# Differential attention in two 64-row halves, with the stacks of terms written to DRAM and one causal mask moved to GpSimd

## The chip, the cores and the metric

The kernel runs on one core of a Trainium2 chip. The metric is the device time of one execution in microseconds (us), the median of several executions. The engines are TensorE (PE, with its weight loads as PEld), VectorE (DVE), ScalarE (ACT), GpSimd (POOL) and SyncE (SP), whose queue (SPq) issues all DMA transfers of this kernel.

## The reference

Sixteen sequences of 256 tokens and 256 channels pass through eight sublayers: four pairs of an attention and a feed-forward part, each behind a layer norm and with a gated residual. The change touches the third sublayer, called L1_attn: a differential attention with 32 heads of 8 channels, whose softmaxes are subtracted in pairs.

```
scaling = HD ** (-0.5)
q = (x @ Wq).reshape(b, t, 2 * H, HD).transpose(0, 2, 1, 3) * scaling
k = (x @ Wk).reshape(b, t, 2 * H, HD).transpose(0, 2, 1, 3)
v = (x @ Wv).reshape(b, t, H, 2 * HD).transpose(0, 2, 1, 3)
scores = jnp.einsum('bhqd,bhkd->bhqk', q, k)
causal = jnp.triu(jnp.full((t, t), -jnp.inf, dtype=jnp.float32), 1)
aw = jax.nn.softmax((scores + causal).astype(jnp.float32), axis=-1)
...
aw = aw.reshape(b, H, 2, t, t)
aw = aw[:, :, 0] - lam * aw[:, :, 1]
attn = jnp.einsum('bhqk,bhkd->bhqd', aw, v)
attn = attn * jax.lax.rsqrt(jnp.mean(attn * attn, axis=-1, keepdims=True) + 1e-05)
...
return attn @ Wo
```

## The kernel before

Each sublayer is a loop of slots over the 16 sequences (`slots`); all residual rows X stay in SBUF. Every engine has its own program for the slot, and semaphores tie them together. A step for a later sequence stands in an earlier slot: in slot i of L1_attn, k and q are projected for sequence i+1, the maxima are taken for sequence i, the second half of the heads (groups gg 4 to 7) of sequence i-1 is finished, and then the first half (gg 0 to 3) of sequence i is taken up to its values product.

The scores are computed twice, from bf16. Each f32 q and k is split into three bf16 parts (`split_qk` on POOL, qk_parts), the parts go to DRAM (qk_dram, L2232), and 24 transfers of 8 rows each bring them back into the stacks QS and KS (L2249): six products of parts, 8 channels each, are 48 contraction rows for one head of a pair, and rows 64 to 111 hold the other head of the pair. QS has a separate column block for each head of the pair, with zeros in the other head's rows, so that all matmuls contract over 128 rows. Two more transfers (L2251) clear three rows for the maximum.

- `max_scores` (PE, L1881 to L1890) makes the scores with queries on partitions, for four heads: one bank with the first query tile, two banks with the second; `later4` is added by a matmul with the identity as the causal mask. `maxima` (DVE, L2105) takes the negated row maxima, `split_max` (POOL, L2196 to L2202) splits them into three bf16 parts, `max_T` (PE, L1898) transposes them, ACT copies them to maxT (L2025), and SP writes them into three rows of QS (`l1a_max_sync`, L2263: six transfers for each half of the heads).
- `exp_scores` (PE, L1920 to L1927) makes the scores again with keys on partitions, now with the maximum subtracted by the matmul itself, and the mask `earlier4`; ACT takes the exponent (`exps`, L2036) into pw (first key tile, 256 queries) and pz (second key tile, 128 queries).
- `values` (PE, L1942 and L1944) multiplies with v in 32-column pieces; `by_token` transposes to tokens and DVE divides (L2113, L2115); `subtract`, squares (POOL, L2213), mean (DVE), the power -0.5 (POOL, L2217), `norm`, `normed_T`, `out` (L1971), `gated` (DVE, L530) and `add_to_x` (POOL, L535) end the sublayer for the sequence. `ln_rstd` (POOL, L485 and L487) belongs to the layer norm of a later sequence.

The order of work on an engine is only the order of the calls in its `slot`. On SP a slot is: the gate's transfer (L522), the parts of sequence i+1 to DRAM (`l1a_sync`), then, behind a wait for the first maxT of sequence i, six L2263 transfers, 26 transfers for the stacks of sequence i+1 (`l1a_stack_sync`), and, behind the second maxT, six more L2263 transfers.

## Time and profile before

| | us |
|---|---|
| three runs, median | 2285.53 |
| three runs, lowest to highest | 2275.45 to 2287.73 |
| the profiled execution | 2258.67 |
| its span | 2256.8 |

| engine | busy us | share of the span |
|---|---|---|
| PE | 1910.5 | 85% |
| PEld | 1418.4 | 63% |
| DVE | 1373.3 | 61% |
| POOL | 896.1 | 40% |
| ACT | 762.5 | 34% |

The busy shares are means over eight sublayers with different limits. L1_attn covers about 643 to 1420 us of the span. The mean granted clock of TensorE is 0.925 of full speed over the span. In the rows further on, a timeline has the start in us, the duration in us, the engine, the line, the operation, what is written and read, how many, and in brackets how long the engine had stood idle and on whose account.

### The profile page before, as it was taken

The numbers are of one execution on the slowest core, as the hardware profiler recorded it, in microseconds if no ns is written. First come the engines' busy times: TensorE is split into PE (matmuls) and PEld (weight loads), VectorE is DVE, ScalarE is ACT, GpSimd is POOL, SyncE is SP. The second block draws the span as 40 slices with busy tenths as digits, with TensorE's granted clock in tenths as the row PEclk, the third lists the DMA queues.
The fourth block names the chain that finished last, engine by engine and source line by source line (L and its number), as shares of the span: only waits on it lengthen the run. The fifth ranks groups of instructions, "written<-read, shape, count | busy, mean of one in ns | idle before, by whom it ended". The sixth has DMA issues, their size and how long they took to land.

```text
span 2256.8 us, 41632 instructions
## 1 busy us (share of the span) xinstructions
PE 1910.5 (85%) x13912; PEld 1418.4 (63%) x13912; DVE 1373.3 (61%) x3587; ACT 762.5 (34%) x1575; POOL 896.1 (40%) x917
## 2 busy tenths in 40 slices
PE   8999997899956887888898967798986787998887
PEld 5655554789944666566666645576765666886343
DVE  4777775565523554445445534688874676887775
ACT  2444443122212454444454534011112222443332
POOL 0354455665541344333443422133334222664333
PEclk9999998999988999899999989799999888999787
DMA  6100000100025344334433430000000100000011
GB/s 221 41 8 7 5 7 8 32 8 9 10 38 108 48 62 63 49 61 56 64 65 54 66 57 5 10 10 7 9 21 27 36 14 21 10 14 15 28 36 43
DMA packets 116497, 82.05 MB, mean 36 GB/s; under 512 B 10524, under 2 KB 113676, under 8 KB 116108
## 3 DMA queue, kind: packets, MB, share of 16 engines
q1 hardware_dynamic: 116364, 80.22, 17.6%
q8 instruction: 91, 1.49, 0.3%
q14 instruction: 42, 0.34, 0.1%
HBM read 62.49 MB, written 16.91 MB: 35 GB/s over the span
## 4 chain that ended last, share of the span: by engine, by line
PE 54%; SPq 16%; DVE 16%; issue 6%; DMA 4%; POOL 2%; ACT 1%; DVEq 1%; POOLq 0%; ACTq 0%
PE PS L1017 15%; SPq L2249 10%; SPq L2263 5%; DMA QS<-maxT 3%; PE PS L665 3%; PE PS L722 2%; PE PS L1172 2%; PE PS L738 2%; DVE xn L494 2%; PE PS L504 2%; PE PS L1920 2%; PE PS L719 2%; PE PS L1889 1%; PE PS L689 1%; PE PS L1942 1%
## 5 line engine op out<-in xcount | busy, mean ns | idle before, releaser
L2105 DVE TENSOR_REDUCE negmax<-PS 128x2 f32<-128x512 f32 (+1 forms) x384 | 241.3, 684 | 275.7 <-PE PS L1884 275.1
L535 POOL TENSOR_TENSOR X<-X,y_sb 128x512 f32 (+1 forms) x128 | 165.4, 1292 | 205.9 <-DVE y_sb L530 200.9
L2036 ACT ACTIVATE pw<-PS 128x512 f32<-128x512 f32 x256 | 140.1, 595 | 261.9 <-PE PS L1921 261.5
L530 DVE TENSOR_TENSOR y_sb<-PS,ga_sb 128x512 f32<-128x512 f32 x96 | 66.4, 692 | 245.5 <-PE PS L1971 71.9
L1920 PE MATMUL PS<-QS,KS 128*128 128x256 bf16 x512 | 104.8, 285 | 89.5 <-DMA QS<-maxT 89.5
L1017 PE MATMUL PS<-we_hi,h_parts 128*128 128x512 f32 x512 | 177.0, 406 | 0.0
L494 DVE TENSOR_SCALAR xn<-X,mv,rs 128x256 f32 (+1 forms) x256 | 157.7, 657 | 22.8 <-POOL rs L487 21.5
L514 ACT ACTIVATE hT<-PS,modT 128x256 f32<-128x256 f32 x256 | 130.0, 558 | 108.9 <-PE PS L504 107.8
L1017 PE MATMUL PS<-l_h_parts,lut_hi 128*128 128x256 f32 (+1 forms) x768 | 143.0, 288 | 6.7 <-POOL l_h_parts L1140 6.7
L485 POOL TENSOR_TENSOR rs<-mv,eps 128x2 f32<-128x2 f32 x128 | 26.8, 210 | 297.3 <-DVE mv L478 297.1
L1506 DVE SCALAR_TENSOR_TENSOR l_acc<-PS,rt_g,l_acc 128x256 f32<-128x256 f32 x256 | 105.9, 475 | 25.6 <-PE PS L1017 21.7
L1017 PEld LDWEIGHTS PS<-l_h_parts,lut_hi 128*128 128x128 f32 (+1 forms) x768 | 115.6, 181 | 9.3 <-issue 5.2
L1920 PEld LDWEIGHTS PS<-QS,KS 128*128 128x128 bf16 x512 | 51.8, 101 | 107.5 <-issue 57.5
L1017 PEld LDWEIGHTS PS<-we_hi,h_parts 128*128 128x128 f32 x512 | 97.4, 190 | 25.3 <-issue 5.3
L1017 PE MATMUL PS<-l_h_parts,lut_lo 128*128 128x256 f32 (+1 forms) x384 | 108.8, 283 | 0.0
L504 PE MATMUL PS<-ident,xn 128*128 128x128 f32 x512 | 81.2, 282 | 32.5 <-DVE xn L494 32.5
L1889 PE MATMUL PS<-KS,QS 128*128 128x256 bf16 x512 | 107.8, 288 | 1.1 <-ACT l_vpad L2066 0.3
L1017 PE MATMUL PS<-we_lo,h_parts 128*128 128x512 f32 x256 | 101.5, 397 | 0.0
L1890 PE MATMUL PS<-later,ident_b 128*128 128x128 bf16 x512 | 98.7, 228 | 0.0
L1172 PE MATMUL PS<-hT,l_wqkv 128*128 128x256 f32 x384 | 94.2, 397 | 4.9 <-ACT hT L514 4.0
L487 POOL TENSOR_TENSOR rs<-rs,half 128x2 f32<-128x2 f32 x128 | 94.2, 736 | 10.0
L1921 PE MATMUL PS<-earlier,ident_b 128*128 128x128 bf16 x512 | 97.4, 227 | 0.0
(270 smaller groups left out, 4806.4 us busy)
## 6 DMA issues: line engine op xcount, KB each, us to landing
ga_sb<-ga_dram SPq DMA_DIRECT2D x128, 128.0 KB, 2.9
qk_dram<-qk_parts SPq DMA_DIRECT2D x16, 768.0 KB, 4.1
QS<-qk_dram SPq DMA_DIRECT2D x192, 64.0 KB
KS<-qk_dram SPq DMA_DIRECT2D x192, 64.0 KB
wmod<-in_wmod SPq DMA_DIRECT2D x4, 1536.0 KB, 13.4
y_out<-X SPq DMA_DIRECT2D x16, 256.0 KB, 2.2
...
```

What stands on the lines that cost most here:

```text
L494: last_ = dve.tensor_scalar(xn[b.par][:, t, :], xb(b)[:, t, :], mv[b.par][:, t, 0:1], rs[b.par][:, t:t + 1], ALU.subtract, ALU.mult)
L504: last_ = pe.transpose(PS[:, 0, kh * T + t * P:kh * T + (t + 1) * P], xn[b.par][:, t, kh * P:(kh + 1) * P], ident[:, :])
L514: last_ = act.activation(hT[b.par][:, kh, :], PS[:, 0, kh * T:(kh + 1) * T], ACT.Identity, bias=modT[:, sub, 0, kh, bass.ds(b.n, 1)], scal ...
L535: pool.tensor_tensor(xb(b), xb(b), y_sb[b.par][:, :, :], ALU.add).then_inc(s.x.sem, 1)
L1017: last_ = pe.matmul(out, x.bitcast(F32R), y.bitcast(F32R), start=start and n == 0, stop=stop and n == 2)
L1172: last_ = pe.matmul(bank(1 + n)[:, m * T:(m + 1) * T], l3_wqkv[:, kh, n * D + m * P:n * D + (m + 1) * P], hT[b.par][:, kh, :], start=kh == ...
L1889: pe.matmul(o, q_of(b, h, P, T), k_of(b, h, 0, T), start=True, stop=False)
L1920: pe.matmul(o, k_of(b, h, 0, P), q_of(b, h, 0, T), start=True, stop=False)
L2036: act.activation(to.rearrange("p a n -> p (a n)"), bank(4 + n), ACT.Exp).then_inc(s.prob.sem, 1)
L2105: dve.tensor_reduce(to, src, AX.X, ALU.max, negate=True).then_inc(s.max.sem, 1)
L2249: sp.dma_start(to, src).then_inc(stack_in[i.par], 16)
L2263: sp.dma_start(QS[b.par][r0:r0 + 1, 8 * half_:8 * half_ + 8, pr, :], maxT[half_][r1:r1 + 8, :])\
```

## The change

Only L1_attn is changed, and the place of the first feed-forward part's buffers in SBUF.

- The rows of Wq and Wk are permuted, so that the parts of one half of the heads lie on 64 neighbouring partitions. `l1a_sync` writes the stacks whole to DRAM, all six terms, with the repeats that the six products need: 12 transfers a slot in place of one. `l1a_stack_sync` then reads them with four transfers of 48 rows (in place of 24 of 8 rows and two of zeros), and `l1a_max_sync` needs two transfers for each half in place of six.
- QS loses its doubled columns. `max_pair` and `exp_pair` work on two heads (pr 0 and 1) with contraction over 48 or 64 rows each, one in partitions 0 to 63 and one in 64 to 127, alternating, and into two different banks. A unit is a bank; a pair of units comes at once, and three banks rotate.
- The mask of the second key tile is not added by a matmul any more: `cut` on POOL zeroes the entries behind the exponent with affine_select, one for each pz buffer, eight a slot, with a small tensor_tensor ahead of each that carries the wait. `values` waits for `cut`.
- `values` and `copy_oT` work on 8 heads at a time, four times a slot in place of eight. pw and pz are doubled.
- The projections, transposes and the output product use bank 0. The end of a sequence (norm, `normed_T`, `out`, `gated`, `add_to_x`) moves to the slot after, so there is one more slot. `split_qk` is done for k and q apart.

The diff, cut; ACT's program follows PE's order and is left out:

```diff
-        QS, KS = wbuf("QS", [P, 16, 2, T], 2, BF16), wbuf("KS", [P, 16, T], 2, BF16)
+        QS, KS = wbuf("QS", [P, 16, T], 2, BF16), wbuf("KS", [P, 16, T], 2, BF16)
...
+        N_TERMS, Q_RUNS, K_RUNS = 6, ((0, 3, 0, 0), (3, 5, 1, 0), (5, 6, 2, 0)), ((0, 3, 0, 1), (3, 5, 0, 1), (5, 6, 0, 0))
...
+            def max_pair(b, o, n):
+                u = 6 * o + 2 * n
...
+                if u >= 2:
+                    pe.wait_ge(*s.max(b, u - 1))
+                elif (b - 1).ok:
+                    pe.wait_ge(*s.max(b - 1, 23))
+                banks = [bank(1 + (u + pr) % 3) for pr in range(2)]
+                if n == 0:
+                    for pr in range(2):
+                        pe.matmul(banks[pr], ident_b[:, :], later4[:, :, :], start=True, stop=False)
+                    for j in range(4):
+                        for pr in range(2):
+                            last_ = pe.matmul(banks[pr][:, j * P:(j + 1) * P], half_rows(q, pr, 4 * o + j, 0, P, M_ROW),
+                                              half_rows(k, pr, 4 * o + j, 0, P, M_ROW), start=False, stop=j == 3)
+                            if j == 3:
+                                last_.then_inc(s.max_ps.sem, 1)
+                else:
+                    for j in range(2):
+                        for pr in range(2):
+                            g = 4 * o + 2 * (n - 1) + j
+                            pe.matmul(banks[pr][:, j * T:(j + 1) * T], half_rows(q, pr, g, P, T, M_ROW),
+                                      half_rows(k, pr, g, 0, T, M_ROW), start=j == 0, stop=False)
+                    for pr in range(2):
+                        pe.matmul(banks[pr].rearrange("p (j k) -> p j k", j=2)[:, :, P:T], ident_b[:, :], later4[:, 0:2, :],
+                                  start=False, stop=True).then_inc(s.max_ps.sem, 1)
...
+            def exp_pair(b, o, n):
...
+                banks = [bank(4 + (u + pr) % 3) for pr in range(2)]
+                if n < 2:
+                    for j in range(2):
+                        for pr in range(2):
+                            g = 4 * o + 2 * n + j
+                            pe.matmul(banks[pr][:, j * T:(j + 1) * T], half_rows(k, pr, g, 0, P, 64),
+                                      half_rows(q, pr, g, 0, T, 64), start=j == 0, stop=False)
+                    for pr in range(2):
+                        pe.matmul(banks[pr].rearrange("p (j q) -> p j q", j=2)[:, :, 0:P], ident_b[:, :], earlier4[:, 0:2, :],
+                                  start=False, stop=True).then_inc(s.score.sem, 1)
+                else:
+                    for j in range(4):
+                        for pr in range(2):
+                            last_ = pe.matmul(banks[pr][:, j * P:(j + 1) * P], half_rows(k, pr, 4 * o + j, P, T, 64),
+                                              half_rows(q, pr, 4 * o + j, P, T, 64), start=j == 0, stop=j == 3)
+                            if j == 3:
+                                last_.then_inc(s.score.sem, 1)
...
+            def values(b, o):
+                pe.wait_ge(*s.prob(b, 6 * o + 4))
+                pe.wait_ge(*s.cut(b, 2 * o + 2))
...
+            def slot(i):
+                c, d, e = i + 1, i - 1, i - 2
+                if i.ok:
+                    max_pair(i, 0, 0)
+                if c.ok:
+                    project_k(c)
+                if d.ok:
+                    exp_pair(d, 2, 0)
+                    exp_pair(d, 2, 1)
+                if i.ok:
+                    max_pair(i, 0, 1)
+                if d.ok:
+                    values(d, 1)
+                    exp_pair(d, 2, 2)
+                if i.ok:
+                    max_pair(i, 0, 2)
+                if c.ok:
+                    project_q(c)
+                if d.ok:
+                    exp_pair(d, 3, 0)
+                if i.ok:
+                    max_pair(i, 1, 0)
+                if d.ok:
+                    values(d, 2)
+                    exp_pair(d, 3, 1)
+                if i.ok:
+                    max_pair(i, 1, 1)
+                if d.ok:
+                    exp_pair(d, 3, 2)
+                if i.ok:
+                    max_pair(i, 1, 2)
+                if e.ok:
+                    normed_T(e)
+                if i.ok:
+                    max_pair(i, 2, 0)
+                    max_T_first(i)
+                if d.ok:
+                    values(d, 3)
+                if i.ok:
+                    max_pair(i, 2, 1)
+                if c.ok:
+                    project_v(c)
+                if i.ok:
+                    max_pair(i, 2, 2)
+                if d.ok:
+                    by_token(d)
+                if i.ok:
+                    exp_pair(i, 0, 0)
+                    max_pair(i, 3, 0)
+                if e.ok:
+                    out(e)
+                if i.ok:
+                    for n in (1, 2):
+                        exp_pair(i, 0, n)
+                        max_pair(i, 3, n)
+                next_tokens(i)
+                if i.ok:
+                    exp_pair(i, 1, 0)
+                    values(i, 0)
+                    max_T_second(i)
+                    exp_pair(i, 1, 1)
+                    exp_pair(i, 1, 2)
+            slots(pe, slot, -2, LOOP2, B + 1)
...
+            def slot(i):
+                d, e = i - 1, i - 2
                 ahead(ln_stats, dve, pl, i, 3)
+                if i.ok:
+                    for n in range(3):
+                        maxima(i, 0, n)
+                if e.ok:
+                    norm(e)
+                if i.ok:
+                    for n in range(3):
+                        maxima(i, 1, n)
+                ahead(ln_apply, dve, pl, i, 2)
+                if i.ok:
+                    for n in range(3):
+                        maxima(i, 2, n)
+                if d.ok:
+                    by_token(d)
+                    subtract(d)
+                if i.ok:
+                    maxima(i, 3, 0)
+                if e.ok:
+                    dve.wait_ge(*s.y_ps(e))
+                    gated(dve, pl, s, e, bank(0).rearrange("p (t d) -> p t d", t=TT))
+                if i.ok:
+                    for n in (1, 2):
+                        maxima(i, 3, n)
+                if d.ok:
+                    mean_square(d)
+            slots(dve, slot, -3, LOOP2, B + 1)
...
+            def split_qk(b, c, n):
+                hi, mid, lo = (qk_parts[b.par][:, a, c, :] for a in range(3))
+                pool.wait_ge(*(s.k if c else s.q)(b))
...
+            def cut(b, o):
+                for pr in range(2):
+                    pool.wait_ge(*s.prob(b, 6 * o + 5 + pr))
+                    pool.tensor_tensor(cut_spare[:, 2 * o + pr:2 * o + pr + 1], zero[:, :], zero[:, :], ALU.add)
+                    pool.affine_select(pz[o % 2][pr][:, :, :], pz[o % 2][pr][:, :, :], pattern=[[0, 4], [1, P]],
+                                       compare_op=ALU.is_ge, fill=0.0, base=0, channel_multiplier=-1).then_inc(s.cut.sem, 1)
+            def squares(b):
+                pool.wait_ge(*s.att(b))
+                pool.tensor_tensor(l1_sq[:, :, :], l1_att[:, :, :], l1_att[:, :, :], ALU.mult).then_inc(s.sq.sem, 1)
+            def root(b):
+                pool.wait_ge(*s.ms(b))
+                pool.tensor_tensor(l1_ms[:, :], l1_ms[:, :], eps_sum1[:, 0:TT * HEADS], ALU.add).then_inc(s.rn_raw.sem, 1)
+                pool.wait_ge(*s.rn_raw(b))
+                pool.tensor_tensor(l1_ms[:, :], l1_ms[:, :], half[:, 0:TT * HEADS], ALU.pow).then_inc(s.rn.sem, 1)
             def slot(i):
                 ahead(ln_rstd, pool, pl, i, 3)
                 if (i + 1).ok:
+                    split_qk(i + 1, 1, 0)
+                if (i - 1).ok:
+                    cut(i - 1, 2)
+                if (i + 1).ok:
+                    split_qk(i + 1, 0, 2)
+                if (i - 1).ok:
+                    cut(i - 1, 3)
                 if i.ok:
                     split_max(i, 0)
                 if (i - 1).ok:
+                    squares(i - 1)
+                if i.ok:
+                    cut(i, 0)
+                if (i - 2).ok:
+                    add_to_x(pool, pl, s, i - 2)
                 if i.ok:
                     split_max(i, 1)
+                    cut(i, 1)
                 if (i - 1).ok:
+                    root(i - 1)
+            slots(pool, slot, -3, LOOP2, B + 1)
...
+        def l1a_sync(sp, pl, s, b):
+            for c, runs in ((1, K_RUNS), (0, Q_RUNS)):
+                sp.wait_ge(*s.parts(b, 2 - c))
+                for r in range(2):
+                    for n0, n1, part, step in runs:
+                        src = qk_parts[b.par][64 * r:64 * r + 64, part:part + (n1 - n0 if step else 1), c, :]
+                        if not step:
+                            src = src.broadcast_to([P // 2, n1 - n0, KH * T])
+                        sp.dma_start(qk_dram[b.par, c, r, n0:n1].rearrange("n p x -> p n x"), src).then_inc(scratch_in[b.par][c], 16)
         def l1a_stack_sync(sp, pl, s, i):
...
+            for c in (1, 0):
+                if not c or not (i - 1).ok:
+                    sp.wait_ge(*scratch_ready(i, c))
+                for r in range(2):
+                    to = (QS, KS)[c][i.par][64 * r:64 * r + M_ROW, :, :].rearrange("p g t -> p (g t)")
+                    sp.dma_start(to, qk_dram[i.par, c, r].rearrange("n (d g) x -> (n d) (g x)", d=8)).then_inc(stack_in[i.par], 16)
...
+                    sp.wait_ge(*scratch_ready(b + 1, 1))
+                r0, r1 = 64 * pr + M_ROW, 24 * pr
+                sp.dma_start(QS[b.par][r0:r0 + 3, 8 * half_:8 * half_ + 8, :], maxT[half_][r1:r1 + 24, :])\
+                  .then_inc(max_in[b.par], 16)
...
```

The SP queue inside one slot, before: parts to DRAM (qk_dram), six maximum rows, the stacks, six more maximum rows, the gate.

```order
L2232 DMA qk_dram<-qk_parts 128x12x256
L2263 DMA QS<-maxT 1x8x256 x6
L2249 DMA QS<-qk_dram 8x16x256 x6
L2249 DMA KS<-qk_dram 8x16x256 x6
L2251 DMA QS<-in_no_max 3x16x256
L2249 DMA QS<-qk_dram 8x16x256 x6
L2249 DMA KS<-qk_dram 8x16x256 x6
L2251 DMA QS<-in_no_max 3x16x256
L2263 DMA QS<-maxT 1x8x256 x6
L522 DMA ga_sb<-ga_dram 128x256
```

The same place after the change, from the q half of the parts on:

```order
L2352 DMA qk_dram<-qk_parts 64x3x512
L2352 DMA qk_dram<-qk_parts 64x2x512
L2352 DMA qk_dram<-qk_parts 64x512
L2376 DMA QS<-maxT 3x8x256 x2
L2365 DMA KS<-qk_dram 48x4096 x2
L2365 DMA QS<-qk_dram 48x4096 x2
L2376 DMA QS<-maxT 3x8x256 x2
L527 DMA ga_sb<-ga_dram 128x256
```

The 24 stack transfers became four, the twelve maximum transfers four, and the gate's transfer stays behind them; ahead of them stand twelve transfers to DRAM in place of one.

POOL from the power on l_ms over the end of a slot into the next one, before:

```order
L2217 TENSOR_TENSOR l_ms<-l_ms,half 128x32
L2196 TENSOR_TENSOR mparts<-negmax,zero 128x2x2x8
L2198 TENSOR_TENSOR m_rest<-negmax,mparts 128x32
L2200 TENSOR_TENSOR mparts<-m_rest,zero 128x2x2x8
L2202 TENSOR_TENSOR mparts<-m_rest,mparts 128x2x2x8
L535 TENSOR_TENSOR X<-X,y_sb 128x512
L485 TENSOR_TENSOR rs<-mv,eps 128x2
L487 TENSOR_TENSOR rs<-rs,half 128x2
L2179 TENSOR_TENSOR qk_rest<-qk,qk_parts 128x1024
L2181 TENSOR_TENSOR qk_parts<-qk_rest,zero 128x1024
L2183 TENSOR_TENSOR qk_parts<-qk_rest,qk_parts 128x1024
L2196 TENSOR_TENSOR mparts<-negmax,zero 128x2x2x8
```

The same stretch after the change (cut_spare and AFFINE_SELECT are `cut`, in the first rows of the next slot for the group o = 2 of the sequence before):

```order
L2310 TENSOR_TENSOR l_ms<-l_ms,eps_sum 128x32
L2312 TENSOR_TENSOR l_ms<-l_ms,half 128x32
L490 TENSOR_TENSOR rs<-mv,eps 128x2
L492 TENSOR_TENSOR rs<-rs,half 128x2
L2272 TENSOR_TENSOR qk_rest<-qk,qk_parts 128x512
L2274 TENSOR_TENSOR qk_parts<-qk_rest,zero 128x512
L2276 TENSOR_TENSOR qk_parts<-qk_rest,qk_parts 128x512
L2300 TENSOR_TENSOR cut_spare<-zero 128x1
L2301 AFFINE_SELECT pz_0<-pz_0 128x512
L2300 TENSOR_TENSOR cut_spare<-zero 128x1
L2301 AFFINE_SELECT pz_1<-pz_1 128x512
L2272 TENSOR_TENSOR qk_rest<-qk,qk_parts 128x512
```

The power now stands at the very end of a slot, directly ahead of `ln_rstd`, the k split and two selections; before, the second `split_max` and `add_to_x` stood between.

PE at the last exponent unit of a group and the values product behind it, before:

```order
L1921 MATMUL PS<-earlier,ident_b 128x128
L1923 MATMUL PS<-earlier,ident_b 128x512
L1927 MATMUL PS<-QS,KS 128x128 x4
L1942 MATMUL PS<-pw_0,l_vpad 32x256 x2
L1942 MATMUL PS<-pw_1,l_vpad 32x256 x2
L1944 MATMUL PS<-pz,l_vpad 32x128 x4
```

PE after the change around the values product of the group o = 2 (pw_0, pz_0 and pw_1, pz_1 are the two halves), in a slot ahead of the loop:

```order
L1884 MATMUL PS<-later,ident_b 128x512 x2
L1887 MATMUL PS<-KS,QS 128x128 x8
L1966 MATMUL PS<-pw_0_0,l_vpad 32x256 x2
L1966 MATMUL PS<-pw_0_1,l_vpad 32x256 x2
L1968 MATMUL PS<-pz_0,l_vpad 32x128 x4
L1966 MATMUL PS<-pw_1_0,l_vpad 32x256 x2
L1966 MATMUL PS<-pw_1_1,l_vpad 32x256 x2
L1968 MATMUL PS<-pz_1,l_vpad 32x128 x4
L1940 MATMUL PS<-QS,KS 128x256 x4
L1943 MATMUL PS<-earlier,ident_b 128x2x128 x2
L1895 MATMUL PS<-KS,QS 128x256 x4
L1898 MATMUL PS<-later,ident_b 128x2x128 x2
```

The mask matmul of the second key tile is gone, the score matmuls of the two halves alternate in one run, and matmuls with 64 contraction rows, with 128 (masks) and with 32 output rows (values) follow each other.

## Rows read from the trace of the kernel before

**Rows 1.** The page: the chain that ended last, share of the span by line.
```profile
PE PS L1017 15%; SPq L2249 10%; SPq L2263 5%; DMA QS<-maxT 3%; PE PS L665 3%; PE PS L722 2%; PE PS L1172 2%; PE PS L738 2%; DVE xn L494 2%; PE PS L504 2%; PE PS L1920 2%; PE PS L719 2%; PE PS L1889 1%; PE PS L689 1%; PE PS L1942 1%
```

**Rows 2.** Timeline of SP's queue, one slot (start us, us, engine, line, operation).
```profile
920.17 4.86 SPq L2263 DMA_DIRECT2D QS<-maxT  x6
...
944.05 4.21 SPq L2263 DMA_DIRECT2D QS<-maxT  x6
```

**Rows 3.** Timeline of PE around the start of one slot.
```profile
904.84 0.39 PE L1920 MATMUL PS<-QS,KS 128*128 128x256 bf16 x1 [6.78 <-DMA QS<-maxT]
...
907.75 0.27 PE L1889 MATMUL PS<-KS,QS 128*128 128x256 bf16 x1
```

**Rows 4.** Timeline of SP's queue: transfers after maxT, first and last slot.
```profile
696.32 4.22 SPq L2263 DMA_DIRECT2D QS<-maxT  x6
...
1366.67 22.72 SPq L2263 DMA_DIRECT2D QS<-maxT  x12
```

**Rows 5.** Timeline of PE: scores of four heads, then the values product.
```profile
880.86 0.39 PE L1884 MATMUL PS<-KS,QS 128*128 128x128 bf16 x4
881.09 0.27 PE L1889 MATMUL PS<-KS,QS 128*128 128x256 bf16 x1
881.19 0.22 PE L1890 MATMUL PS<-later,ident_b 128*128 128x128 bf16 x1
...
882.62 0.39 PE L1927 MATMUL PS<-QS,KS 128*128 128x128 bf16 x4
882.94 0.64 PE L1942 MATMUL PS<-pw,l_vpad 128*32 128x256 f32 x8
883.39 0.40 PE L1944 MATMUL PS<-pz,l_vpad 128*32 128x128 f32 x8
883.73 0.39 PE L1881 MATMUL PS<-later,ident_b 128*128 128x512 bf16 x1
```

**Rows 6.** Timeline of PE at the end of a slot: the projections.
```profile
894.44 1.89 PE L1843 MATMUL PS<-hT,l_wk 128*128 128x256 f32 x8
896.17 1.89 PE L1843 MATMUL PS<-hT,l_wq 128*128 128x256 f32 x8
```

**Rows 7.** Timeline of POOL over one slot.
```profile
967.28 0.26 POOL L2196 TENSOR_TENSOR mparts<-negmax,zero 128x32 bf16<-128x32 f32 x1 [8.59 <-DVE negmax L2105]
...
968.27 0.25 POOL L2202 TENSOR_TENSOR mparts<-m_rest,mparts 128x32 bf16<-128x32 f32 x1
976.37 1.04 POOL L2213 TENSOR_TENSOR l_sq<-l_att 128x512 f32<-128x512 f32 x1 [7.86 <-DVE l_att L2121]
...
979.42 5.44 POOL L2217 TENSOR_TENSOR l_ms<-l_ms,half 128x32 f32<-128x32 f32 x1
...
990.98 1.28 POOL L535 TENSOR_TENSOR X<-X,y_sb 128x512 f32 x1 [4.62 <-DVE y_sb L530]
992.21 0.20 POOL L485 TENSOR_TENSOR rs<-mv,eps 128x2 f32<-128x2 f32 x1
992.48 0.71 POOL L487 TENSOR_TENSOR rs<-rs,half 128x2 f32<-128x2 f32 x1
994.50 2.12 POOL L2179 TENSOR_TENSOR qk_rest<-qk,qk_parts 128x1024 f32<-128x1024 f32 x1 [1.31 <-ACT qk_parts L2053]
996.70 1.89 POOL L2181 TENSOR_TENSOR qk_parts<-qk_rest,zero 128x1024 bf16<-128x1024 f32 x1
```

**Rows 8.** All POOL groups by shape: a memset, count, busy us, mean ns.
```profile
L2162 POOL MEMSET l_vpad<- 128x1024 f32 x2 | 1.8, 956 | 0.0
```

**Rows 9.** Timeline of DVE: a division by token, then three maxima.
```profile
971.25 0.26 DVE L2113 RECIPROCAL l_rl<-PS 128x16 f32<-128x16 f32 x1 [3.48 <-PE PS L1954]
...
973.75 1.88 DVE L2105 TENSOR_REDUCE negmax<-PS 128x4 f32<-128x512 f32 x3
```

**Rows 10.** Timeline of ACT: two exponents in a row.
```profile
963.13 1.09 ACT L2036 ACTIVATE pw<-PS 128x512 f32<-128x512 f32 x2 [1.12 <-PE PS L1921]
```

**Rows 11.** The chain in order of time: the last transfer before the first slot.
```profile
676.16 9.22 DMA QS<-in_no_max
```

446 lines of the change are left out of this document (183 added, 263 removed).

## The prediction

> **What bounds the kernel now.** I read the page's chain first: behind PE stands SP's queue, with two lines of L1_attn alone at 15% of the span and the landing of QS<-maxT at 3% [rows 1]. So this sublayer runs at the pace of its transfers. SP's timeline shows a slot of it: from the first maxT six issues take 4.9 us, the 26 issues of the stacks fill the time up to 944.05, and six more take 4.2 us [rows 2]; together 28.1 us. The scores of the next group wait for these rows: PE stands 6.8 us and resumes at 904.84 [rows 3]. Its matmuls then take 0.39 us where the same form takes 0.27 us in a busy stretch [rows 3, 5], and are back at 0.27 at 907.75: the granted clock had fallen to the lower of its two levels, 1.2 GHz, while PE stood. About 1.5 us are lost by that. A slot lasts 44.7 us: (1366.67 - 696.32) / 15 [rows 4]. Everything below is a sum for one slot, times 15, plus the ends.
>
> **What goes away.** The chain from a maxT to the exponents. After the change two issues of 0.7 us follow each maxT (six took 4.2 to 4.9 [rows 2]), and four issues replace the 26. Even if each large transfer lasted three times an old issue, SP would be free within 5 us, and the landing is covered by over 20 us of work on PE between the first maxT and the next slot. Twelve issues to DRAM stand ahead of the maxT wait; at 0.7 us they are 8.4 us, half of them while POOL splits q. I cost SP at nothing. If that cover failed, the 6.8 us of [rows 3] would come back. The gate's transfer now stands behind the second maxT and its rows; `gated` needs it a slot later, so it costs nothing. So the question is which engine is late next.
>
> **PE.** A 256-column score matmul has a pitch of 0.10 us, four of 128 columns 0.23 us (880.86 to 881.09) [rows 5]. Before, a group of four heads costs 2.2 us in scores and 0.8 in values. Two halves in flight at once would halve the score part but not the masks. The trace has no matmul with 64 contraction rows; the nearest rows are the values products, which use 32 of the columns each: eight records of 256 columns in 0.45 us [rows 5], where eight records of 256 columns over the full array take 1.73 us [rows 6]. So disjoint tiles do overlap here, and I take full overlap for the halves: a pair of exponent or maximum units with masks is 0.2 + 0.2 us. But entering and leaving the 32-column form costs 0.10 us: four 128-column matmuls start at 882.62, and the values not at 882.84 but at 882.94; leaving (883.39 to 883.73) shows 0.12 more than the 0.22 of its columns [rows 5]. After the change the form switches twice in each pair, so a pair is 0.55 to 0.65 us. Sum for PE: about 15 us scores, 6 values, 10 others (four projections at 1.73 [rows 6] among them), 31 us a slot, with 28 to 36 as bounds. The Trainium skill, in "TensorEngine Tiling (Array Packing)", section Tiling Modes, says that changing the tiling mode drains the engine, which speaks against mixing 64-row scores and 128-row masks; the 0.10 us above agree with it. PE is not late by this. Bank 0 now serves projections, transposes and the output product in turn; between any two of them the order puts at least a pair of units, 0.6 us, about the length of one eviction, so I cost that at nothing too.
>
> **POOL.** The selection is what the trace does not show. Its bounds: a memset writes 1024 columns in 0.96 us, 0.48 for 512 [rows 8]; two passes of the square over 512 columns would be 2.1 us (1.04 each [rows 7]). I take 1.04, the square of the same shape and type, near to half of the one-input pass over 1024 (1.89 [rows 7]). With 0.20 for the small operation ahead (that of two columns [rows 7]) and 0.06 of gaps, one `cut` buffer is 1.3 us, a pair 2.6, a slot 10.4. The Trainium skill, in "GPSIMD Engine Reference", section Performance versus the Vector engine, gives 0.77 us for a tight one-input loop over 512 elements; no row here shows it, and by it the slot below would be 2.2 us shorter and the kernel within 0.5% of now.
>
> POOL's busy time would be about 28 us, less than a slot; the matter is its order. `root` stands last in a slot, behind cut(i,1), and ahead of `ln_rstd`, the k split and cut(d,2); and values(d,2) on PE waits for that cut. Behind that wait stands all that PE does for DVE and ACT, so both run dry with it. So I walk one slot round along what waits for what, beginning when the last exponent unit of sequence i is in PSUM:
> 1. first exponent 0.55 (1.09 for two [rows 10]) and handover, then cut(i,1): 0.65 + 2.6 = 3.25
> 2. root 0.25 + 0.08 + 5.44, then rstd 0.20 + 0.07 + 0.71 [rows 7], together 6.9; the k split, three passes over 512: fixed 0.2 plus half the rest of 2.12, 1.89 and 2.12 gives 3.4, with gaps 3.6 [rows 7]: 10.5
> 3. cut(d,2): 2.6
> 4. PE: values 2 x (0.45 + 0.22) + 0.1, exponent units 0.6, wait for their first exponent, the last pair 0.5, its first exponent 0.65: 4.0
> 5. cut(d,3): 2.6
> 6. split_max(i,0), from 967.28 to 968.52 [rows 7]: 1.25
> 7. PE: max_T 0.3, values 1.45, a pair 0.55, the v projection 1.75, a pair and its latency 0.75: 4.8
> 8. DVE: two maxima at 0.6 (1.88 for three) and handover 1.25, then four divisions 2.5 (971.25 to 973.75) [rows 9]: 3.75
> 9. PE: pairs 0.6 + 0.85, out 1.75, then 0.6 + 0.6 + 0.6; first exponent 0.65: 5.65
> 10. cut(i,0): 2.6
> 11. add_to_x 1.3 and split_max(i,1) 1.3 [rows 7]: 2.6
> 12. PE: max_T 0.3, two pairs with the exponent between them: 2.0
> The sum is 45.6 us, of which 10.4 are selections. No queue of the chip can go round this faster, since each step waits for the one ahead. Between PE's arrival at values(d,2) and step 3's end it stands some 5 us (its own work up to there, max, k, three exponent pairs, values, q, is about 11 us, POOL's 16.4), nearly as long as now, so I add the same 1.5 us of low clock: 47.1 us, against 44.7.
>
> **The ends.** At the start the last stack transfer now lands at 685.4 (676.16 + 9.22 [rows 11]); the 26 issues' 19 us [rows 2] become about 3, so 16 us earlier. At the end one more slot has to be passed with root, norm, out: about 4 us more than now. Sum: 15 x 2.4 - 16 + 4 = +24 us on the profiled execution's 2258.67, so 2283, 1.1% more. The median of the runs shown, 2285.5, lies 1.2% above the profiled execution; the same ratio on it gives **2310**.
>
> **The rivals.**
> A. The selection is cheap. At the memset's 0.48 us the walk is 45.6 - 8 x 0.56 = 41.1, with the clock 42.6: 15 x (-2.1) - 12 = -44, 2241. Half way, at 0.8 us, it is about -15. For it: a selection reads one input and writes one. Against it: even plain one-input passes on POOL take about 1.0 us here [rows 7]. It decides from 0.85 us downward. Chance 0.26.
> B. POOL's order does not bind, because the path has slack that I don't see, or operations of 512 columns are cheaper than by my halving. Then PE's 31 us with waits for PSUM banks (about 0.35 us at ten alternations, and the waits of steps 8) hold: 38 us a slot, -112 us, 2174. For it: SP's 28 us are gone in any case, and POOL is only 40% busy now. Against it: root, split and cut stand in one queue and PE waits by name for cut. Chance 0.10.
> C. The selection takes two passes, 2.1 us: the walk is 54.1, with the clock 55.6, so +150, 2436 (slower). Against it: no row of a select. It needs only a compare and a choice done after each other. Chance 0.12.
> D. The halves don't run beside each other, that is, the change doesn't do what it says: each pair on PE costs 0.2 more, nine or ten of them lie on the path: 49 us, +55, 2341. For it: the alternate matmuls need weight loads in between and switches to the mask form. Chance 0.12.
> My forecast (selection 0.9 to 1.3 us, halves overlapping): 2283 on the profiled execution, its own range 2265 to 2305 there, 2292 to 2332 on the median. Chance 0.40.
>
> **How the numbers follow.** About 0.5% (11 us) is what a measurement of this kernel can tell from no change. Faster by over 0.5%: A mostly (0.24), B (0.10), the lower edge of the forecast (0.02): 0.36. Within 0.5%: 0.14, the edge of A and of the forecast. Slower: C, D and the rest of the forecast, 0.50. The range has to take in A's end at the memset, 2241 on the profile and 2268 on the median, with a little of B, and C's end nearly whole: 2205 to 2435.
>
> **What the profile after would show.** SPq no longer in the chain; POOL with lines of `cut` and root in it. The selection's mean decides between the forecast, A and C. PE's idle time ahead of the values lines should be laid to affine_select and be about 5 us a slot ahead of the group o = 2; if it is laid to DMA, SP's cover failed. In a pair, the matmuls of the two halves should start within a few hundredths of a us of each other; if they follow at 0.1 us, D holds. A slot, from one first maxT to the next, should be 47 us. It would be wrong as a whole if POOL stands idle at the turn of a slot.

## The result, and the profile after

The change makes the kernel faster: 2222.01 us, median of four executions (2219.28 to 2223.03), against 2280.49 us for the kernel before beside it (2273.18 to 2287.73), a ratio of 0.9742 with a 95% interval of 0.9703 to 0.9781. The prediction was 2310 us, slower. Its range (2205 to 2435) held the time; its sign and the price that it put on the selection did not hold. What came true is the mechanism of its rival A, the cheap selection.

The page of the changed kernel, busy times and the chain that ended last (compare [rows 1]):

```profile
span 2219.6 us, 40110 instructions
PE 1857.4 (84%) x13272; PEld 1279.4 (58%) x13272; DVE 1378.1 (62%) x3587; ACT 750.2 (34%) x1511; POOL 994.2 (45%) x1221
...
PE 54%; DVE 17%; issue 16%; POOL 8%; ACT 2%; DMA 2%; SPq 1%; DVEq 1%; POOLq 0%; ACTq 0%
PE PS L1022 15%; PE PS L670 3%; PE PS L727 3%; PE PS L1177 2%; PE PS L743 2%; PE PS L509 2%; PE PS L1966 2%; DVE xn L499 2%; PE PS L724 2%; PE PS L1843 1%; POOL pz L2301 1%; PE PS L694 1%; PE PS L771 1%; DVE negmax L2181 1%; DVE rt_eq L1367 1%
```

SP's queue, 15% of the span in two lines before, is down to 1%, and POOL stands at 8% with the selection (L2301) as a line of its own. POOL's busy time rose by 98 us, and the kernel is faster nevertheless.

The selection, in the groups of the stretch 700 to 1300 us (line, engine, operation, output and input, count, busy us, mean ns, idle before), beside the power:

```profile
L2312 POOL TENSOR_TENSOR l_ms<-l_ms,half 128x32 f32<-128x32 f32 x13 | 70.7, 5438 | 1.0
L2301 POOL TENSOR_SCALAR_AFFINE_SELECT pz<-pz 128x512 f32<-128x512 f32 x110 | 69.7, 634 | 0.0
L2300 POOL TENSOR_TENSOR cut_spare<-zero 128x1 f32<-128x1 f32 x109 | 21.0, 192 | 126.3 <-ACT pz L2101 126.3
```

One selection takes 0.634 us, where the sum had 1.04. The turn of a slot on POOL, the same kernel's timeline (compare [rows 7]):

```profile
911.57 0.25 POOL L2310 TENSOR_TENSOR l_ms<-l_ms,eps_sum 128x32 f32<-128x32 f32 x1
911.90 5.44 POOL L2312 TENSOR_TENSOR l_ms<-l_ms,half 128x32 f32<-128x32 f32 x1
917.31 0.19 POOL L490 TENSOR_TENSOR rs<-mv,eps 128x2 f32<-128x2 f32 x1
917.58 0.70 POOL L492 TENSOR_TENSOR rs<-rs,half 128x2 f32<-128x2 f32 x1
918.25 1.16 POOL L2272 TENSOR_TENSOR qk_rest<-qk,qk_parts 128x512 f32<-128x512 f32 x1
919.48 1.37 POOL L2274 TENSOR_TENSOR qk_parts<-qk_rest,zero 128x512 bf16<-128x512 f32 x1
920.93 1.15 POOL L2276 TENSOR_TENSOR qk_parts<-qk_rest,qk_parts 128x512 bf16<-128x512 f32 x1
922.04 0.19 POOL L2300 TENSOR_TENSOR cut_spare<-zero 128x1 f32<-128x1 f32 x1
922.18 0.63 POOL L2301 TENSOR_SCALAR_AFFINE_SELECT pz<-pz 128x512 f32<-128x512 f32 x1
922.78 0.19 POOL L2300 TENSOR_TENSOR cut_spare<-zero 128x1 f32<-128x1 f32 x1
922.92 0.63 POOL L2301 TENSOR_SCALAR_AFFINE_SELECT pz<-pz 128x512 f32<-128x512 f32 x1
923.52 1.16 POOL L2272 TENSOR_TENSOR qk_rest<-qk,qk_parts 128x512 f32<-128x512 f32 x1
```

POOL has no gap from the root through both selections of group 2 and the q split: the queue that the prediction described is there. One `cut` buffer takes (923.52 - 922.04) / 2 = 0.74 us, where the sum had 1.3. PE at the same place:

```profile
923.68 0.64 PE L1966 MATMUL PS<-pw,l_vpad 128*32 128x256 f32 x8 [2.59 <-POOL pz L2301]
...
925.68 0.61 PE L1940 MATMUL PS<-QS,KS 64*128 64x256 bf16 x4
926.23 0.61 PE L1943 MATMUL PS<-earlier,ident_b 128*128 128x256 bf16 x2
...
928.81 0.39 PE L1898 MATMUL PS<-later,ident_b 128*128 128x256 bf16 x2
```

It stands 2.59 us for the selection, and by 925.68 the granted clock is at its lower level (0.61 us for a form that takes 0.39 us at the higher one); by 928.81 it is back. Before, PE stood at the turn of this slot for 6.78 us, and for a DMA [rows 3].

SP's queue, the first and the last slot's transfers behind the first maxT, and one slot in the middle (compare [rows 2, 4]):

```profile
685.54 1.68 SPq L2376 DMA_DIRECT2D QS<-maxT  x2
...
922.11 8.78 SPq L2352 DMA_DIRECT2D qk_dram<-qk_parts  x12
932.66 1.66 SPq L2376 DMA_DIRECT2D QS<-maxT  x2
934.44 0.80 SPq L2365 DMA_DIRECT2D KS<-qk_dram  x2
935.28 0.89 SPq L2365 DMA_DIRECT2D QS<-qk_dram  x2
952.65 1.48 SPq L2376 DMA_DIRECT2D QS<-maxT  x2
...
1323.28 20.39 SPq L2376 DMA_DIRECT2D QS<-maxT  x4
```

A slot lasts (1323.28 - 685.54) / 15 = 42.5 us, against 44.7 before. The difference of the spans (2219.6 and 2256.8), -37.2 us, splits in three: the slots give 15 x -2.17 = -32.6 us, the first maxT comes 10.8 us earlier (685.54 for 696.32), and the rest of the span takes 6.2 us more.

The mean of 42.5 hides that the slots are not alike. From one first maxT to the next, the first slot, which has no sequence before it to finish, takes 32.3 us (685.54 to 717.82), and the last 38.9 us (1284.37 to 1323.28); before, these two took 44.4 and 44.1 us. The 13 slots between take 43.6 us on average, for 44.8 before. So over half of the 32.6 us, 17.3, comes from two slots, and a full slot became only 1.2 us shorter.

A pair of exponent units on PE in the change:

```profile
904.21 0.39 PE L1940 MATMUL PS<-QS,KS 64*128 64x256 bf16 x4
904.54 0.39 PE L1943 MATMUL PS<-earlier,ident_b 128*128 128x256 bf16 x2
```

Four matmuls of 256 columns and the switch to the mask's form take 0.33 us. One after the other the four alone would take about 0.4 us, at the pitch of 0.10 us that such a matmul had before [rows 5].

### The profile page after: what moved, and what is told of

Read it like the earlier page. It is cut to its first block, busy times and chain, and to the rows that moved or that the text cites. A ratio compares the mean times of both kernels' runs of the same rounds, so it can differ in the third digit from the quotient of the medians.

```text
span 2219.6 us, 40110 instructions
## 1 busy us (share of the span) xinstructions
PE 1857.4 (84%) x13272; PEld 1279.4 (58%) x13272; DVE 1378.1 (62%) x3587; ACT 750.2 (34%) x1511; POOL 994.2 (45%) x1221
## 4 chain that ended last, share of the span: by engine, by line
PE 54%; DVE 17%; issue 16%; POOL 8%; ACT 2%; DMA 2%; SPq 1%; DVEq 1%; POOLq 0%; ACTq 0%
PE PS L1022 15%; PE PS L670 3%; PE PS L727 3%; PE PS L1177 2%; PE PS L743 2%; PE PS L509 2%; PE PS L1966 2%; DVE xn L499 2%; PE PS L724 2%; PE PS L1843 1%; POOL pz L2301 1%; PE PS L694 1%; PE PS L771 1%; DVE negmax L2181 1%; DVE rt_eq L1367 1%
## 5 line engine op out<-in xcount | busy, mean ns | idle before, releaser
L2181 DVE TENSOR_REDUCE negmax<-PS 128x2 f32<-128x512 f32 (+1 forms) x384 | 247.2, 685 | 324.2 <-PE PS L1898 200.5
L1966 PE MATMUL PS<-pw,l_vpad 128*32 128x256 f32 x1024 | 89.1, 419 | 36.4 <-POOL pz L2301 20.9
L2300 POOL TENSOR_TENSOR cut_spare<-zero 128x1 f32<-128x1 f32 x128 | 24.6, 193 | 159.6 <-ACT pz L2101 159.6
L1091 ACT ACTIVATE l0f_act<-PS 128x256 f32<-128x256 f32 x96 | 36.8, 383 | 175.0 <-PE PS L1022 175.0
L478 DVE BATCH_NORM_STATS2 st<-X 128x6 f32 (+1 forms) x256 | 95.1, 413 | 1.1 <-DMA X<-in_x 0.8
L1154 POOL TENSOR_TENSOR l0f_hid_parts<-l0f_hid,l0f_hid_parts 128x256 fp32r<-128x256 f32 x96 | 72.2, 753 | 50.4 <-DVE l0f_hid_parts L1016 50.0
```

Source lines behind the costliest of these rows:

```text
L478: last_ = dve.bn_stats(st6[b.par][:, t, :], xb(b)[:, t, :])
L1966: pe.matmul(to, v, pw[o % 2][pr][j // 2][:, j % 2, :], start=True, stop=False)
L2181: dve.tensor_reduce(to, src, AX.X, ALU.max, negate=True).then_inc(s.max.sem, 1)
```

## The experiments

Each kernel ran beside the kernel before on the same chip, and its ratio to it is the number that compares across the groups of runs, since the median of before lay between 2266 and 2284 us in them. "Slot" is taken as above, from SP's timeline.

| kernel | median us | ratio (95% interval) | slot us |
|---|---|---|---|
| before | 2280.49 | 1 | 44.7 |
| the change | 2222.01 | 0.9742 (0.9703 to 0.9781) | 42.5 |
| sel_twice | 2319.4 | 1.0223 (1.0176 to 1.027) | 48.3 |
| sel_none | 2165.2 | 0.9534 (0.9489 to 0.9579) | 38.8 |
| mask_mm | 2157.42 | 0.9523 (0.9477 to 0.9569) | 38.7 |
| before_dma | 2187.15 | 0.9638 (0.9595 to 0.968) | 40.6 |
| root_early | 2240.83 | 0.9829 (0.9765 to 0.9894) | 43.6 |
| root_mask_mm | 2235.85 | 0.9806 (0.9741 to 0.9871) | 43.3 |
| root_gap | 2209.71 | 0.9669 (0.9613 to 0.9725) | 41.5 |
| gap_mask_mm | 2184.46 | 0.9574 (0.9521 to 0.9627) | 40.1 |
| halves_apart | 2222.45 | 0.975 (0.9684 to 0.9815) | 42.6 |
| one_half | 2280.02 | 0.9967 (0.9933 to 1.0001) | 45.7 |
| stack_24 | 2267.1 | 0.9942 (0.9904 to 0.998) | 45.1 |

Two theories stood at first. The first: POOL's queue sets the slot, with all eight selections on its path. The rival: PE's own work sets it, and the selections lie beside it.

**sel_twice**, a second selection of the same size ahead of each:

```diff
+                    pool.affine_select(cut_more[:, 2 * o + pr, :, :], pz[o % 2][pr][:, :, :], pattern=[[0, 4], [1, P]],
+                                       compare_op=ALU.is_ge, fill=0.0, base=0, channel_multiplier=-1)
                     pool.affine_select(pz[o % 2][pr][:, :, :], pz[o % 2][pr][:, :, :], pattern=[[0, 4], [1, P]],
```

> After with a second selection of each pz buffer into a spare tile, ahead of the real one; nothing else changes. Theory 1 (POOL's order sets the slot, eight selections lie on its path): 8 x 0.60 us more a slot, 15 slots, +72 us, about 2294 us. Theory 2 (PE's work and its waits for PSUM banks set the slot; POOL stands idle some 18 us of it): the second selections go into POOL's idle time, at most +20 us, 2222 to 2242 us.

Measured 4.8 points more than the change (97 us between the two medians), and 5.7 us a slot for eight selections at a pitch of about 0.6 us (4.8 us). The path takes all of them, and something on top, which fits the waits of PE for them (stretch 700 to 1300: us in total, times, longest); of the change first, then of sel_twice:

```profile
PE PS L1966 <- POOL pz L2301: 20.6, 8, 2.9
```

```profile
PE PS L1967 <- POOL pz L2304: 45.5, 16, 4.9
PE PS L1906 <- POOL mparts L2295: 34.9, 23, 2.4
```

The low clock is more frequent too: the mean granted clock of sel_twice is 0.904, the change's 0.921.

**sel_none**, the selection left out (the small operation signals in its place):

```diff
-                    pool.tensor_tensor(cut_spare[:, 2 * o + pr:2 * o + pr + 1], zero[:, :], zero[:, :], ALU.add)
-                    pool.affine_select(pz[o % 2][pr][:, :, :], pz[o % 2][pr][:, :, :], pattern=[[0, 4], [1, P]],
-                                       compare_op=ALU.is_ge, fill=0.0, base=0, channel_multiplier=-1).then_inc(s.cut.sem, 1)
+                    pool.tensor_tensor(cut_spare[:, 2 * o + pr:2 * o + pr + 1], zero[:, :], zero[:, :], ALU.add).then_inc(s.cut.sem, 1)
```

> After without the selection; the small operation ahead of it carries the semaphore. The causal mask of the second key tile is left out, so this part of the computation is missing. Theory 1: 8 x 0.60 us less a slot while POOL's path still sets it, down to where PE takes over (38 to 40 us a slot): -40 to -72 us, 2150 to 2182 us. Theory 2: under 15 us less, 2207 to 2222 us.

**mask_mm**, the mask of the second key tile added by a matmul again, and no `cut`:

```diff
+                    for pr in range(2):
+                        pe.matmul(banks[pr], ident_b[:, :], earlier4[:, :, :], start=True, stop=False)
...
-                pe.wait_ge(*s.prob(b, 6 * o + 4))
-                pe.wait_ge(*s.cut(b, 2 * o + 2))
+                pe.wait_ge(*s.prob(b, 6 * o + 6))
```

> After with the mask of the second key tile added by a matmul again (one bank-wide mask matmul for each unit), and no cut on POOL. Theory 1: the path loses four pairs of cuts (5.9 us) and gains the mask matmuls of two groups (2 x 0.55 us): about 37.7 us a slot against 42.5, or PE's own limit of 38: -55 to -70 us, about 2160 us. Theory 2: PE has 4 x 0.55 us more to do in a slot: +33 us, 2255 us.

Both give 38.7 to 38.8 us a slot, 3.7 less than the change; eight selections of 0.6 us would be 4.8, so taken away they are not all on the path: the next bound is met about 1 us earlier. In mask_mm PE is busy 519 of the 600 us, and what waits are left are short and spread over ACT's exponents, POOL's split maxima and DVE; no run takes one of them away, so this bound is read from the trace and not tested. The longest of them:

```profile
PE PS L1940 <- ACT pw L2102: 16.6, 16, 1.2
PE PS L1905 <- POOL mparts L2295: 16.5, 16, 1.1
```

The two ratios differ by 0.1 points, the medians by 0.4%, mask_mm being the faster: the eight mask matmuls of 512 columns, which the selection was to save, cost nothing that shows. mask_mm is the fastest kernel of this study, 2.2 points below the change.

**before_dma**, the kernel before with the new transfers alone (permuted weights, stacks whole in DRAM, four transfers of 48 rows and two of zeros back, two for each maxT), its full-array scores and mask matmuls kept:

```diff
-            for pr in range(2):
-                for c, terms in ((0, Q_TERMS), (1, K_TERMS)):
-                    for n, part in enumerate(terms):
...
+            for c in (1, 0):
+                for r in range(2):
+                    to = KS[i.par][64 * r:64 * r + M_ROW, :, :] if c else QS[i.par][64 * r:64 * r + M_ROW, :, r, :]
+                    sp.dma_start(to, qk_dram[i.par, c, r].rearrange("n (d g) (m t) -> (n d) (g m) t", d=8, m=KH)).then_inc(stack_in[i.par], 16)
```

> Before with the new way of the transfers alone: permuted weights, whole stacks to DRAM in 12 transfers, four of 48 rows and two of zeros back, two for each half of the maxima. All compute instructions and their order are those of before. If SP's 28 us set the slot of before, it falls to PE's 35 us of work and some waits, 37 to 39 us from 44.7: -85 to -115 us on before's 2280, about 2180, below after. Rival: the time of before lies in its order of work, or the large transfers land late: less than 20 us gained, 2260 or more.

The transfers alone bring more (-3.6%) than the whole change (-2.6%). With mask_mm this splits the change in three: transfers 1 - 0.9638 = -3.6%, all else but the selection (halves, whole-group values, new order) 0.9638 - 0.9523 = -1.2%, the selection 0.9742 - 0.9523 = +2.2%. The middle part is itself a difference: one_half, below, puts the overlap of the halves alone at 2.2 points in the changed kernel, so that the rest of that part (order of work, whole-group values, one more slot) may cost about a point; no run has it alone. In before_dma the landing of QS<-maxT still ends PE's waits, with 30.7 us in all in place of 65.0; the 6.8 us that the prediction quotes was the longest of 27. The row of the kernel before, then of before_dma:

```profile
PE PS L1920 <- DMA QS<-maxT: 65.0, 27, 6.8
```

```profile
PE PS L1924 <- DMA QS<-maxT: 30.7, 15, 2.7
```

**root_early**, `root` ahead of the selections of group 0 in place of the end of the slot (and `mean_square` behind the maxima of (3,0)):

```diff
                 if (i - 1).ok:
                     squares(i - 1)
+                    root(i - 1)
                 if i.ok:
                     cut(i, 0)
...
-                if (i - 1).ok:
-                    root(i - 1)
```

> The changed kernel with two moves in the order of work and nothing left out: the mean of the squares stands on DVE right behind the maxima of (3,0), and the root (5.8 us on POOL) right behind the squares, ahead of the selections of group 0. The theory that POOL's order sets the slot takes root's 5.8 us out of the turn of the slot and puts about 1 us in its place between the squares and the selections of group 0 (the squares come early enough that PE works on meanwhile): slot 42.5 -> 38 to 39 us, about -55 us, near 2165. The rival, that the slot is set by PE's own matmuls and the low clock, expects 2210 to 2230, no change. If root only shifts the wait from the selections of group 2 to those of group 0, the slot loses about 2 us: near 2190.

It got slower by 0.9 points, where a gain was expected. The timeline of PE shows why:

```profile
917.52 1.08 PE L1966 MATMUL PS<-pw,l_vpad 128*32 128x256 f32 x8 [3.61 <-POOL pz L2301]
```

The 5.8 us only stand ahead of another selection: PE now waits 3.61 us for group 0's, where it waited 2.59 us for group 2's, and the low clock follows there. POOL in turn idles 2.47 us at the turn of the slot.

**root_mask_mm**, the same move in mask_mm:

> The changed kernel with the mask of the second key tile by matmul (no selections) and with root moved as in root_early. With the mask by matmul the slot was already 38.7 us and PE no longer waited for POOL at the turn, so the theory expects little of the second move here: 0 to -15 us against 2157, so 2142 to 2157. If root were what set the slot and the selections only added to it, the move would bring its full 5.8 us a slot: near 2075.

Slower again, and more telling: 2.8 points above mask_mm, although no selection is there to be delayed. The wait that grew is PE's for the split maxima of the second half, which `split_max(i, 1)` makes behind `root` in POOL's queue:

```profile
PE PS L1905 <- POOL mparts L2295: 55.5, 27, 3.3
```

It was 16.5 us in mask_mm. So the late end-of-slot place was better than the early one, whatever it costs.

**root_gap**, `root` a slot later, in POOL's gap of 9.4 us ahead of the squares, with `norm` and `normed_T` moved to match; **gap_mask_mm**, the same in mask_mm:

```diff
                 if i.ok:
                     split_max(i, 0)
+                if (i - 2).ok:
+                    root(i - 2)
                 if (i - 1).ok:
                     squares(i - 1)
```

> The changed kernel, nothing left out, with root one slot later: on POOL root(i-2) stands right behind split_max(i,0), where the changed kernel's trace shows POOL idle for 9.4 us ahead of the squares; norm goes behind the maxima of group 2 on DVE, normed_T ahead of the unit (3,0) on PE. root_early showed root's 5.8 us costing the slot wherever a selection and split_max(i,1) are queued behind it. If the queue order of POOL is the whole matter, root now delays nothing: the wait of 2.6 us ahead of the values of group 2 and most of the low clock behind it go, the slot falls from 42.5 (44.4 in the loop) by 3 to 4 us: -45 to -60, 2162 to 2177. The rival, that a slot of this kernel is bound by PE's own hand-overs with DVE and ACT and any movement of root costs, expects 2220 or more.

> mask_mm (mask of the second key tile by matmul, no selections) with root placed as in root_gap. In mask_mm POOL no longer stands ahead of PE at the turn of a slot, so by the theory nothing of the 5.8 us is on the path there: no change, 2150 to 2165. If root still delayed the k split and with it the stacks' terms, it would gain up to 15 us: 2142. root_mask_mm lost 79 us against mask_mm; if that came from split_max(i,1) standing behind root, it must all be gone here.

root_gap's waits for POOL pz are gone from the list, but the slot falls only by 1.0 us where 3 to 4 were expected. gap_mask_mm shows where the rest went: the same move costs mask_mm, which had nothing to gain, 1.4 us a slot. `norm` now stands on DVE ahead of the divisions by token, and PE's wait for these, and for DVE ahead of the first maxima of group 2, has grown; rows of root_gap, then of gap_mask_mm and mask_mm:

```profile
PE PS L1980 <- DVE l_t L2192: 16.0, 14, 1.2
PE PS L1884 <- DVE negmax L2182: 12.6, 14, 0.9
```

```profile
PE PS L1981 <- DVE l_t L2193: 17.2, 15, 1.2
PE PS L1884 <- DVE negmax L2183: 10.2, 15, 0.7
```

```profile
PE PS L1981 <- DVE l_t L2192: 8.8, 15, 0.6
PE PS L1884 <- DVE negmax L2182: 4.0, 15, 0.7
```

In that stretch of some 15 slots they grew by 8.4 and 6.2 us in the mask_mm pair, together 1.0 of the 1.4 us a slot. The second may cost nothing: `normed_T` no longer stands ahead of that unit, so PE comes to it earlier. The rest was not traced. So freeing POOL's turn is worth about 1.0 + 1.4 = 2.4 us a slot, if the move's own cost adds up in the same way in both kernels, which was not tried apart.

**halves_apart**, the matmuls of the two halves one half after the other:

```diff
-                    for j in range(4):
-                        for pr in range(2):
+                    for pr in range(2):
+                        for j in range(4):
```

> The changed kernel with the score matmuls of the two 64-row halves issued one half after the other, in place of alternating; same operations, same masks. If alternating halves do run beside each other, each pair of units now costs 0.2 us more on PE; nine or ten pairs lie between waits on the path of a slot, so +2 us a slot, +30 us: near 2250. If the halves never overlapped, or the engine overlaps them in this order too, nothing changes: 2215 to 2230. In the trace a pair of 2 x 4 matmuls of 128 columns should take 0.45 us to the mask behind it in place of 0.24.

No change in time, and none in the trace: eight matmuls of 128 columns are followed by the next after 0.23 us in this order too:

```profile
921.94 0.41 PE L1948 MATMUL PS<-QS,KS 64*128 64x128 bf16 x8
922.17 0.40 PE L1895 MATMUL PS<-KS,QS 48*128 48x256 bf16 x4
```

That left two readings open: the halves run beside each other in any order of issue, or a short contraction is faster by itself. **one_half** tells them apart; every score matmul reads the lower half, so the scores of the other heads are left out:

```diff
-                return x[64 * pr:64 * pr + rows, g, a:b_]
+                return x[0:rows, g, a:b_]
```

> The changed kernel with every score matmul reading partitions 0 to 63 (the heads pr = 0 twice; the scores of the other half are left out), same number and shape of matmuls, into the same banks. halves_apart left open why eight matmuls of 128 columns take 0.23 us in either order: either the two row halves run beside each other even when one half's four are issued first, or a matmul with 48 or 64 contraction rows simply takes half the time of one with 128. If the halves' overlap is the reason, it is gone here: a pair takes 0.43 to 0.45 us to the next operation, some ten pairs a slot lie between waits, +2 us a slot, near 2250. If short contractions are fast by themselves, the pair stays at 0.23 us and the time at 2215 to 2230.

The pair takes 0.45 us, and the whole gain of the change is gone (2280 us, 45.7 us a slot):

```profile
903.10 0.62 PE L1948 MATMUL PS<-QS,KS 64*128 64x128 bf16 x8
903.55 0.60 PE L1895 MATMUL PS<-KS,QS 48*128 48x256 bf16 x4
```

So it is the overlap of the two row halves, it does not need the alternating order, and it is worth 3.2 us a slot. That is more than the 2 us expected: at 0.2 us each, it would be 16 of the 24 pairs on the path, not ten.

**stack_24**, the four transfers of 48 rows cut into 24 of 8 rows:

```diff
-                    to = (QS, KS)[c][i.par][64 * r:64 * r + M_ROW, :, :].rearrange("p g t -> p (g t)")
-                    sp.dma_start(to, qk_dram[i.par, c, r].rearrange("n (d g) x -> (n d) (g x)", d=8)).then_inc(stack_in[i.par], 16)
+                    for n in range(N_TERMS):
+                        r0 = 64 * r + 8 * n
+                        to = (QS, KS)[c][i.par][r0:r0 + 8, :, :].rearrange("p g t -> p (g t)")
+                        sp.dma_start(to, qk_dram[i.par, c, r, n].rearrange("(d g) x -> d (g x)", d=8)).then_inc(stack_in[i.par], 16)
```

> The changed kernel with its four stack transfers of 48 rows cut into 24 of 8 rows, each row still 8 KB in one piece; same bytes. SP issues about 15 to 20 us more a slot at 0.7 to 0.8 us each. The prediction costed SP at nothing since over 20 us of work on PE cover it: by that no change, 2215 to 2230. If cover was thin and the issues delay the rows of the second maxT, the slot grows: the issues of the stacks stand between the first and the second group of rows of the maxima, 20 us apart, and with 24 issues the second would come up to 5 us late: +75 us, near 2300.

It loses 2.0 points, 2.6 us a slot, but not in the way expected: 24 issues take 8.1 us for 4 transfers' 1.7, and the second maxT's rows are still issued on time. The stacks land later. PE waits for them at the first unit of a slot, a wait that totals 0.2 us in halves_apart, a kernel with the change's transfers; stack_24's wait, one slot of SP, and PE at its end:

```profile
PE PS L1884 <- DMA QS<-qk_dram: 63.3, 12, 12.2
...
883.65 4.09 SPq L2367 DMA_DIRECT2D KS<-qk_dram  x12
887.78 4.05 SPq L2367 DMA_DIRECT2D QS<-qk_dram  x12
...
905.25 1.03 PE L1884 MATMUL PS<-later,ident_b 128*128 128x512 bf16 x2 [3.78 <-DMA QS<-qk_dram]
```

PE goes on 13.4 us after the last issue ended (891.83 to 905.25), and 21.6 us after the first began. In the change the QS transfers land 9.3 us after their issue, so all four are in about 10.6 us after the first began (934.44, the last issue at 935.7):

```profile
QS<-qk_dram SPq DMA_DIRECT2D x32, 384.0 KB, 9.3
```

The bytes are the same. What differs is how fast they move. The last two numbers of these rows are the mean busy share of the 16 DMA engines and GB/s, for stack_24 behind its last issue and for the change while its four transfers run:

```profile
891.80:895.00 3.20, 3.06 (x27) 1.61 (x25) 2.06 (x4) 1.19 (x3) 0.00 (x0) 1.00 0.53 82
```

```profile
939.00:941.00 2.00, 0.61 (x8) 0.18 (x6) 1.90 (x6) 0.00 (x0) 0.00 (x0) 1.00 0.96 156
```

While SP is still issuing (883.6 to 891.8) stack_24 moves 81 to 82 GB/s as well, so it is not the issues that hold it back: transfers of 8 rows keep the DMA engines busy for about half of the time, those of 48 rows for nearly all of it. So the 2.0 points that the 48 rows win come from the rate of the transfers and not through SP's queue. Why 8 rows give half the share stays open; the form of the rows in DRAM was not tried alone.

## Why the prediction was wrong

- **What bounds the kernel before, and that SP's path goes away: right.** SPq is at 1%, the waits of PE that cost most end with POOL, ACT and DVE, and before_dma shows the transfers' worth by themselves. "SP at nothing" held, but only for large transfers: in stack_24 the stacks come 21.6 us after the first issue, and that is already too late by 3.8 us.
- **The halves' overlap and the form switch: right.** A pair of exponent units takes 0.33 us to its mask (the overlapped columns 0.21 and a switch of about 0.11), eight matmuls of 128 columns 0.23 us; one_half shows the opposite case, so rival D is refuted. Its price was too low: 2 us a slot were reckoned, one_half took 3.2. PE is busy 479 of the 600 us from 700 to 1300, 34 us a slot for the 31 reckoned. The Trainium skill, "TensorEngine Tiling (Array Packing)", Tiling Modes, has a mode switch drain the engine; the 0.11 us here agree, in that each switch costs time.
- **The walk round one slot: right in its structure, and lucky in its total.** sel_twice confirms that all eight selections lie on the path. The wait ahead of group 2 was 2.6 us and not 5, which is the four shorter selections between the last exponents and it. With 0.74 us for a `cut` buffer in place of 1.3 it gives 45.6 - 8 x 0.56 = 41.1, with the low clock 42.6; the mean is 42.5. But the walk is one of a full slot, and full slots take 43.6 on average, 44.3 to 44.7 around the one shown here; the first and the last bring the mean down, which the prediction did not reckon with when it took 15 times one slot. Step by step, in the slot shown above: root, `rstd` and the k split 10.5 us (911.57 to 922.04), as reckoned; from the selections of group 2 to those of group 3 5.4 us for 4.0, the low clock being in it; step 9, from 940.61 to the selections of group 0 at 947.93, 7.3 us for 5.65. There the clock falls a second time in this slot, behind PE's wait for the divisions, and the prediction has one such stretch a slot, not two:

```profile
940.61 0.40 PE L1940 MATMUL PS<-QS,KS 64*128 64x256 bf16 x4 [1.39 <-DVE l_t L2191]
942.32 3.28 PE L2005 MATMUL PS<-l_wo,l_ogT 128*128 128x256 f32 x8
```

- **The step that failed is the selection's size**, 1.04 us in step 1, 3, 5 and 10, measured 0.634. I took the square, of the same shape and type, as the nearest row, and called the pass at 1.89 us over 1024 columns a one-input pass. It is none: its row reads `qk_parts<-qk_rest,zero`, a tensor_tensor with two inputs [rows 7], like the square. So no row had a one-input pass with a read; the memset at 0.48 us [rows 8], which reads nothing, bounded the selection from below, and the value lay 0.15 above that bound and 0.41 below the one taken. That the second input makes the difference is likely and not shown: selection and tensor_tensor differ in the operation too. The Trainium skill, "GPSIMD Engine Reference", Performance versus the Vector engine, gives 0.77 us for a tight loop over 512 elements, which it sets against the slower rate of two inputs; the measured 0.634 is shorter still, but nearer to it than to the row that I took. With the small operation ahead, which follows at 0.14 us where 0.26 were reckoned, the error is 8 x 0.56 = 4.5 us a slot, 67 us in all, and decides the sign: 2222 + 67 us is no faster than the kernel before. sel_twice shows from the other side that selections of such a length turn it: eight more of 0.6 us make the kernel slower than before (1.0223).
- **The ends: right in sum, not in parts.** The stacks of the first slot land 16.8 us earlier (659.08 + 9.56 against 685.4), 16 were forecast, but only 10.8 us reach the first maxT. From the last slot's first maxT to the last `add_to_x` of this sublayer it takes 4.9 us longer, for the 4 forecast; another 1.3 us come in the sublayers behind it. What the sum lacks is the short first and last slot.
- **From the profiled execution to the median: wrong.** The sum with the right selection gives 15 x -2.1 - 12 = -44 on 2258.67, so 2215, and the profiled difference is -37. On the medians it is -58. The factor 1.012 assumed that the changed kernel's profiled execution would also lie 1.2% under its median; it lies on it (2222.34 and 2222.01). The profiled execution of before, 2258.67, is shorter than every other one of that kernel (2261 to 2295 us over the groups of runs); why the changed kernel's runs are closer together was not looked into. Two numbers of the prediction are also wrong by its own sum: rival A's 2241 is the value on the median, not on the profile (there it is 2215, and 2268 is neither), and a selection of 0.8 us gives -5, not -15.
- **The rule about POOL's free time: half right.** The prediction said that not POOL's busy time but its order matters. root_early and root_mask_mm show how strongly: moved ahead of other work, the same 5.8 us cost 0.9 and 2.8 points more than at the end of a slot. But its low estimate of the slot without POOL's order, rival B's 38 us, was met at 38.7 as soon as the selections went, with `root` still in its place. So `root` at the turn costs little without the selections, and with them 2.4 us a slot by the root_gap pair, not its 5.8.

The chain of the changed kernel still has 16% "issue" time (in which an engine waited for nothing that the profile shows). Its full slots are not alike: six in a row inside the loop (888.35 to 1155.54) take 44.3 to 44.7 us, the others 41.5 to 44.4, one of them in the loop too. In the six the product L2005 takes up to 3.3 us, in the shortest slots 1.99 (at 812, 856 and 1208 us), so part of the difference is the second stretch of low clock. What brings it about was not tried.
